# Quantised cross-attention stage: TensorE's transposes issued ahead of the next group's scores

## What is computed

```
h1 = ln(x);  x = attn(h1, h1,      a1_...) + x      # 16 heads of 32
h2 = ln(x);  x = attn(h2, context, a2_...) + x
attn:  q, k, v = h @ wq, ctx @ wk, ctx @ wv         # each fake-quantised to 8 bits
       p   = softmax(fq(q) @ fq(k).T * scale)
       out = fq(p) @ fq(v);   return out @ wo + bo
```

## Time and profile before

| | |
|---|---|
| median of the runs | 2921.24 us |
| the profiled execution's own time | 2920.33 us |
| its span, first to last instruction | 2918.5 us |
| mean granted TensorE clock, share of full speed | 0.973 |
| PE busy | 2712.4 us, 93% |
| DVE busy | 1783.6 us, 61% |
| ACT busy | 1454.5 us, 50% |
| POOL busy | 711.0 us, 24% |

### The profile page before, as it was taken

The page is one execution under the profiler, slowest core; times in us unless marked ns, Lnnn a source line. Parts: engine busy times, 40 slices in busy tenths (PEclk is TensorE's granted clock), DMA queues, the critical chain, the costliest instruction groups (busy, mean ns, idle before and its releaser), DMA issues. The chain is left out here.

```text
span 2918.5 us, 55439 instructions
## 1 busy us (share of the span) xinstructions
PE 2712.4 (93%) x18432; PEld 2210.4 (76%) x18432; DVE 1783.6 (61%) x4410; ACT 1454.5 (50%) x3765; POOL 711.0 (24%) x1147
## 2 busy tenths in 40 slices
PE   5799999999999998489999999997999999999997
PEld 4566666666666665289999999997988888888885
DVE  6789999999999997554444443433444444444434
ACT  5577777777777775331111111112455555555554
POOL 1222222222222221132222232321221221222211
PEclk9899999999999999699999999999999999999999
DMA  4443333333333333431212111114111111111111
GB/s 149 82 82 83 83 79 83 80 83 81 85 84 83 79 83 56 114 128 57 79 50 79 65 65 69 61 72 137 51 44 49 52 43 50 50 43 50 50 36 44
DMA packets 337323, 211.07 MB, mean 72 GB/s; under 512 B 275568, under 2 KB 291952, under 8 KB 337264
## 3 DMA queue, kind: packets, MB, share of 16 engines
q1 hardware_dynamic: 337264, 210.34, 26.8%
HBM read 92.84 MB, written 50.33 MB: 49 GB/s over the span
## 5 line engine op out<-in xcount | busy, mean ns | idle before, releaser
L595 ACT ACTIVATE e<-S,bias,qk_scale 128x256 f32<-128x256 f32 x1024 | 563.1, 564 | 65.7 <-DVE e L707 61.6
L690 DVE TENSOR_REDUCE negmax<-S 128x4 f32<-128x1024 f32 x256 | 312.3, 1220 | 103.8 <-PE S L503 102.0
L707 DVE TENSOR_SCALAR e<-e,rsum 128x256 f16<-128x256 f32 x1024 | 292.0, 349 | 2.5
L565 ACT ACTIVATE shifted<-PJ,round_col,inv 128x512 f32<-128x512 f32 x192 | 149.2, 777 | 226.8 <-PE PJ L157 225.8
L148 PE MATMUL PJ<-w_a_wo,oT 128*128 128x512 f32 x512 | 239.3, 612 | 2.6 <-ACT oT L604 1.8
L1828 POOL TENSOR_TENSOR mid_partsB<-mid_actB,mid_partsB 128x256 fp32r<-128x256 f32 x128 | 97.9, 765 | 561.8 <-DVE mid_partsB L1664 561.8
L1828 POOL TENSOR_TENSOR mid_partsA<-mid_actA,mid_partsA 128x256 fp32r<-128x256 f32 x128 | 100.9, 788 | 518.2 <-DVE mid_partsA L1664 518.2
L157 PE MATMUL PJ<-hT,w_a_wq 128*128 128x256 f32 x1536 | 207.0, 293 | 21.3 <-DVE hT L685 17.5
L157 PEld LDWEIGHTS PJ<-hT,w_a_wq 128*128 128x128 f32 x1536 | 194.2, 197 | 35.3 <-issue 35.3
L157 PE MATMUL AG0B<-h_partsB,upB 128*128 128x256 f32 x1536 | 198.9, 286 | 16.1 <-DVE downB L1593 16.1
L595 ACT ACTIVATION_READ_ACCUMULATOR e<-S,bias,qk_scale 128x1 f32 x1024 | 208.8, 204 | 0.0
(11 more groups left out here) (198 smaller groups left out, 5471.0 us busy)
## 6 DMA issues: line engine op xcount, KB each, us to landing
x_in<-in_x_dram SPq DMA_DIRECT2D x16, 512.0 KB, 3.7
ctx_in<-in_ctx_dram SPq DMA_DIRECT2D x16, 512.0 KB, 3.6
mid_dram<-x SPq DMA_DIRECT2D x16, 512.0 KB, 2.7
y_in<-mid_dram SPq DMA_DIRECT2D x16, 512.0 KB, 3.3
kv_in<-in_ctx_dram SPq DMA_DIRECT2D x16, 512.0 KB, 3.4
h_dram<-h3TA SPq DMA_DIRECT2D x16, 512.0 KB, 2.6
k_dram<-k_out SPq DMA_DIRECT2D x16, 512.0 KB, 2.6
part_dram<-x3A SPq DMA_DIRECT2D x16, 512.0 KB, 2.6
```

The costliest lines, as they stand in the source:

```text
L565: nc.scalar.activation(shifted[:, bank, :], PJ[bank][:], ACT.Identity, bias=round_col[:, 0:1], scale=inv[:, d:d + 1]).then_inc(pj_emptied[ ...
L595: nc.scalar.activation(e[:, s, i, :], S[s][:, i // 2, i % 2, :], ACT.Exp, bias=bias[:, s, i:i + 1], scale=qk_scale[:, ph.a:ph.a + 1], accu ...
L690: nc.vector.tensor_reduce(negmax[:, g % 2, :], S[g % 2][:].rearrange("p i q n -> p (i q) n"), AX_X, ALU.max, negate=True).then_inc(max_don ...
L707: nc.vector.tensor_scalar(e16[:, s, i, :], e[:, s, i, :], rsum[:, s, i:i + 1], ROUND16, ALU.mult, ALU.add).then_inc(prob_scaled, 1)
```

## The change

In `pe_phase` the loop that issues a group's transposes now stands ahead of the scores of g+1. TensorE's list of such a group was scores(g+1), transposes, products with v (g-3), fills; it becomes transposes, scores(g+1), products with v (g-3), fills. Nothing is added or removed, the waits of each piece are the same, and no other engine's list changes. Groups without transposes are as before.

```
             def pe_phase(pe, ph, prev, nxt):
                 for g in range(GROUPS):
+                    fills = ph.steps(g)
+                    for name, j in fills:
+                        if kind_of(name) in ("hT", "h2T", "ctxT"):
+                            pe_fill(pe, at(ph.stage, ph.b, name, j))
                     if g + 1 < GROUPS:
                         pe_scores(pe, ph, g + 1)
                     elif nxt:
                         pe_scores(pe, nxt, 0)
-                    fills = ph.steps(g)
-                    for name, j in fills:
-                        if kind_of(name) in ("hT", "h2T", "ctxT"):
-                            pe_fill(pe, at(ph.stage, ph.b, name, j))
                     if g >= 3:
                         pe_pv(pe, ph, g - 3)
```

## The result

The changed kernel takes 2985.18 us, the median of four runs (2972.17 to 2999.1), against 2920.97 before: the ratio is 1.0217, with a 95% interval of 1.0189 to 1.0246. The change makes the kernel 2.2% slower. The forecast was 2984.

What follows compares the result with a forecast made beforehand. In the quantised stage PE and DVE were taken as nearly full, so a delay of either can reach the end. Order 46.5 plus clock 16.5 made 63 us, hence 2984 us (chance 0.47), range 2957 to 3007.

Steps and rivals of the forecast that it cites:

- hT, 1.6 a pass: hT group, 13 times: later maximum delays the turned tile and the fill behind by 1.6 us each, 20.8 us.
- h2T: h2T group, 14 times: late maximum delays probabilities, DMA and products with v; 6 x 1.6 + 8 x 0.38 = 12.6 us.
- ctxT: ctxT group, 14 times: DVE 1.49 us late, mostly absorbed, xhat about 0.4 late; 5.6 us.
- Outside the loop: Six such groups outside the loop: the first at nothing, the other five 1.5 us each, 7.5 us.
- The clock: Longer PE pauses at h2T and hT lower the granted clock: 6.5 us (0 to 15) and 10 us (0 to 19.5).
- if the granted clock falls in all passes: Sign that the prediction is wrong in size: the clock falling in all passes, or in fewer than before.
- (a): Rival: the clock stays as it is and only the order costs, 46.5 us, giving 2968; chance 0.21.
- (b): Rival: the clock falls in every pass at both h2T and hT, 81 us, giving 3002; chance 0.19.
- (c): Rival: DVE's delay is absorbed, only PE's own order costs 0.33 in 41 groups, 13.5 us, giving 2935; chance 0.06.
- (d): Rival: ACT's shift and xhat release the transposes so late that the order has no effect, 2921; chance 0.03.
- (e): Rival: faster, the turned tile coming 0.33 us sooner in 41 groups, 13.5 us, giving 2907; chance 0.04.

Runs made afterwards that it cites:

- The run with VectorE's order altered: Changed kernel with VectorE's turned tile, its cast and low part put ahead of the next group's maximum: 2953.1 us, ratio 1.0109 against the kernel before.
- the run with h2T alone: Kernel before with only the h2T transposes moved ahead of the scores: 2948.58 us, ratio 1.0085.
- hT alone: Kernel before with only the hT transposes moved ahead of the scores: 2966.33 us, ratio 1.0146.

## Why the prediction came out

**The number.** 2984 against 2985.18 is partly luck. The median lies between two levels because the four executions fell two and two; with three at one level it would have been near 2974 or near 2997.

**hT, 1.6 a pass: right.** Measured 1.48; the prediction's own steps (1.02 + 0.44 + 1.17 less 1.12) make 1.51, which it rounded up to 1.6. The mechanism is the one foretold (1.90 us of wait where about 2.0 was said). The run with VectorE's order altered takes that wait away, and so shows its cause.

**h2T: right in the chain.** The maximum is 1.61 us late (1.47 behind the start of the transposes, before 0.14 ahead of it) and the turned tile 1.48, with the products with v waiting for the DMA 1.01 (1.5 foretold), 1.46 in place of 1.60 in a pass at full clock. The DMA wait was over-sized since the exponentials took a part of it first: the scores ahead of these products waited for them (0.45, in the changed kernel and in the run with h2T alone).

**ctxT: right**, 0.33 for 0.4.

**Outside the loop:** 4.5 ahead and 5.4 behind, with the peeled pass and with slower fills; 7.5 was said, and 0.8 to 2.0 for the peeled pass inside the terms of h2T and ctxT. About right. The bounds that the prediction names for these groups give 2960 to 3004; its range is 3 us wider at each end and doesn't say from what.

**The clock: right in kind, wrong in both sizes.** These two terms failed.
At h2T, 6.5 us were set down. In every other pass of the lower level the k2 fill is slow (4.34), and costs nothing: from the h2T transposes to the next hT transposes it is 31.14 us with a slow fill (547.97 to 579.11) and 31.16 without (475.37 to 506.53). VectorE's path is now the longer one and covers it. Even the 1.2 us that such passes lost before is no longer to be lost, and the forecast had taken that in. What I missed is that in the changed kernel the fall seldom comes early enough to slow the transposes themselves: in none of fourteen passes at the lower level, in three at the upper. With hT alone it did so in seven of fourteen, after a pause of 1.98, so the length of this pause by itself does not decide it.
At hT, 10 us were set down and 19.5 as the bound. At the lower level it is 6 x 1.6 = 9.6, as said. At the upper level it is 12 x 2.47 + 1.5 = 31. The bound came from a fill of which only a part was slow (4.48 for 3.13), and that was no bound: a fill that runs wholly at the low clock takes 5.49 for 3.02. By the prediction's own sign ("if the granted clock falls in all passes") it is wrong in size there.

**The two levels were not foretold.** Rivals (a) and (b) of the prediction treated the clock as a matter of more or fewer passes, and gave 2968 and 3002; measured are 2974 and 2997, each in half of the ten executions. The forecast of 2984 lies between and meets the median, not a time. The range held both.
The Trainium skill (TensorE: Matmul & The Clock Gate, The HAM clock gate) says that the windows in which the gate looks at activity run freely and are not started by the kernel. By it, one program can meet them differently from one execution to the next; the two levels of ten executions agree. That a loop keeps to one pattern is what the two traces show: from the loop's fourth pass on, passes of 75.1 us each at one level, and from its second on, 72.6 and 74.16 in turn at the other. What holds the pattern, and what makes an execution start with the one or the other, is open; no run here varied it.

**Rivals (c), (d), (e)** fell. DVE's delay is not absorbed but stands in PE's waits of 1.90 and 1.01 us, and any part alone is slower than the kernel before. Of the turned tiles only ScalarE's of ctxT came sooner, by 0.31 us (3.93 after the start of the fill ahead, before 4.24), and the passes did not wait for it.

## What to carry to other kernels

Where two engines work off lists that were written to match, moving a piece in one list makes the other engine wait in its old order. Here 0.33 us of matmuls moved behind 1.02 became 1.5 us on VectorE, because a maximum that used to be taken in an idle moment now stood between. Before moving a producer, read what the consumer does in the time that it waits, and who is queued behind it.

Look at the single times, not at their median alone: here two levels were two patterns of slow fills, each kept through the loop, and a profile shows one of them only.

## What was not expected of the hardware

One program takes 2974 or 2997 us on the same chip. At the lower level one fill of a pass runs in turn at 2.4 GHz (3.02 us) and partly at 1.2 (4.6), at the upper wholly at 1.2 (5.49), after two pauses of 1.04 and 1.90 us with 1.75 us of work between them.

A pause of 1.02 to 1.46 us, harmless in the changed kernel, had a slow fill behind it in every other pass once the pauses ahead of it were shortened. Keeping the clock at one place moved the fall to another.

A matmul of 128x128 by 128x512 in full f32 shows as two instructions of 0.46 us.
